# Setup and first attention in one block, scores kept in PSUM, one copy and one cast changed

## The reference

```python
mod = silu(c) @ ada_w.T + ada_b
shift_msa, scale_msa, gate_msa, shift_mlp, scale_mlp, gate_mlp = split(mod, 6, axis=1)
h = layernorm(x) * (1 + scale_msa[:, None]) + shift_msa[:, None]
q, k, v = heads(h @ qkv_w.T + qkv_b)               # 16 heads of 16
attn = where(mask_q & mask_k, q @ k.T * 16**-0.5, -1e9)
x = x + gate_msa[:, None] * (softmax(attn) @ v @ proj_w.T + proj_b)
h = layernorm(x) * (1 + scale_mlp[:, None]) + shift_mlp[:, None]
x = x + gate_mlp[:, None] * (gelu(h @ fc1_w.T + fc1_b) @ fc2_w.T + fc2_b)
# second block: shift from cond, attention with 16 heads of 64 and normed q and k,
# then 8 experts of 1024 hidden units, each over its top 1024 tokens
```

## Time and profile before

| what | value |
|---|---|
| median of 3 runs | 2549.15 us (2547.28 to 2550.14) |
| the profiled execution | 2552.78 us, of which 2550.9 us from first to last instruction |
| busy: PE, DVE, ACT, POOL | 2365.1, 1935.8, 1555.7, 1093.7 us |
| mean granted TensorE clock | 0.959 of full speed |
| setup, until its barrier | 0 to 29.4 us |
| attention0 | 29.4 to 510 us |

### The profile page before, as it was taken

One profiled execution on the slowest core, in us unless ns is written; L12 is line 12 of the kernel. 1 busy time (PEld: TensorE's weight loads), 2 busy tenths in 40 slices (PEclk: granted clock), 3 DMA queues, 4 the chain that ended last, 5 costly groups with the idle time before them and its releaser, 6 DMA issues. The chain is left out here.

```text
span 2550.9 us, 67195 instructions
## 1 busy us (share of the span) xinstructions
PE 2365.1 (93%) x24912; PEld 2075.8 (81%) x24912; DVE 1935.8 (76%) x3769; ACT 1555.7 (61%) x2979; POOL 1093.7 (43%) x939
## 2 busy tenths in 40 slices
PE   4999999889999979999999999999999825999997
PEld 3788888679999958888888888888888714999996
DVE  4899999656667668888888888888888767666663
ACT  3888888656666646566556555555555544655553
POOL 3799999700000024434434434434433303355543
PEclk8999999889999989999999999999999957999999
DMA  4111110011011000000000000000000022244322
GB/s 127 37 37 37 38 40 31 24 26 32 21 31 31 29 34 18 16 15 14 16 16 12 16 16 12 16 16 12 16 16 12 18 58 68 68 95 94 91 53 33
DMA packets 86352, 89.21 MB, mean 35 GB/s; under 512 B 26752, under 2 KB 80640, under 8 KB 83584
## 3 DMA queue, kind: packets, MB, share of 16 engines
q1 hardware_dynamic: 73984, 71.10, 9.0%
q0 software_dynamic: 12288, 17.05, 4.1%
HBM read 62.42 MB, written 25.69 MB: 35 GB/s over the span
## 5 line engine op out<-in xcount | busy, mean ns | idle before, releaser
L1050 POOL TENSOR_TENSOR a_rq<-a_vq,minus_half 128x8 f32<-128x8 f32 x256 | 417.3, 1639 | 98.6 <-DVE a_vq L1075 98.6
L994 ACT ACTIVATE a_sq<-a_bqk 128x512 f32<-128x512 f32 x256 | 152.9, 597 | 349.1 <-PE a_bqk L126 349.1
L1045 POOL TENSOR_TENSOR a_rstd<-a_veps,minus_half 128x1 f32<-128x1 f32 x64 | 35.3, 552 | 617.1 <-DVE a_veps L1119 617.1
L124 PE MATMUL a_bqk<-wqk_hi,a_h_lo 128*128 128x512 f32 x512 | 208.5, 407 | 5.1 <-DVE a_h_lo L1091 5.1
L126 PE MATMUL a_bqk<-wqk_hi,a_h_hi 128*128 128x512 f32 x512 | 201.7, 394 | 0.0
L125 PE MATMUL a_bqk<-wqk_lo,a_h_hi 128*128 128x512 f32 x512 | 201.7, 394 | 0.0
L1067 DVE TENSOR_TENSOR a_qk<-a_bqk,a_rq 128x512 f32<-128x512 f32 x256 | 176.0, 688 | 29.7 <-POOL a_rq L1050 29.6
L1812 DVE TENSOR_TENSOR e_u_lo<-e_u,e_u_hi 128x512 fp32r<-128x512 f32 x128 | 88.8, 695 | 127.2 <-ACT e_u_hi L1675 126.5
L1670 ACT ACTIVATE e_u<-e_bu,e_b 128x512 f32<-128x512 f32 x128 | 88.3, 690 | 156.8 <-PE e_bu L126 154.9
L981 ACT COPY a_vs<-a_ba 64x512 f32<-64x512 f32 x256 | 148.8, 581 | 53.7 <-PE a_ba L126 48.9
L1059 DVE TENSOR_REDUCE a_ss<-a_sq 128x8 f32<-128x512 f32 x256 | 174.2, 680 | 2.8 <-ACT a_sq L994 1.0
(11 more groups left out here) (284 smaller groups left out, 8150.7 us busy)
## 6 DMA issues: line engine op xcount, KB each, us to landing
X<-in_x SPq DMA_DIRECT2D x64, 128.0 KB, 2.1
a_gate<-gates_of_rows SPq DMA_DIRECT2D x128, 64.0 KB, 2.5
m_gate<-gates_of_rows SPq DMA_DIRECT2D x32, 256.0 KB, 4.1
tokens<-a_xs SPq DMA_DIRECT2D x64, 128.0 KB, 1.7
out<-a_xs SPq DMA_DIRECT2D x64, 128.0 KB, 1.7
e_w<-in_fc1s SPq DMA_DIRECT2D x8, 1024.0 KB, 5.1
e_w<-in_fc2s SPq DMA_DIRECT2D x8, 1024.0 KB, 4.8
wst<-in_qkv_w SPq DMA_DIRECT2D x16, 128.0 KB, 2.5
```

Of the source, the lines that this page charges most:

```text
L124: tensor.matmul(to, w_lo, x_hi, start=start, stop=False)
L994: nc.scalar.activation(sq[:, n * BK:(n + 1) * BK], b_qk[:, n * BK:(n + 1) * BK], ACT.Square).then_inc(s["sq"], 1)
L1050: nc.gpsimd.tensor_tensor(rq[:, 8 * n:8 * n + 8], vq[:, 8 * n:8 * n + 8], g.mhalf[:, 0:8], ALU.pow).then_inc(s["rq"], 1)
```

## The change

`setup_phase` is gone; its work is in `attention0_phase`, with semaphores of its own for each load.
- SP loads in the order of need: cond, the first two of six parts of `wada`, x of tiles 0 to 3 in one DMA, weights of q, k, v, constants, the projection's weights, the mask, x of tiles 4 to 7, then the rest of `wada`, `wada1` and the biases, then x of tiles 8 to 13. The mask is stored as 2 rows of 4096 bytes, each spread over 64 partitions.
- The four tables of the first attention are made ahead of step 0, each in a PSUM bank of its own; the other six and the gates at step 0, after the v product, in the banks of `a_bpt`, `a_bo` and of the scores.
- DVE makes `mrow` and `hide` at step -2, and `hidden` in eight pieces of one operation, four at step -1 and four at step 0. `vbB` and `pbB` come at steps 3 and 4, the low part of the weights of q, k, v at step -3, that of the projection's at POOL's step 1.
- Several tiles share memory: `wada` and the gate bias lie where `a_PT` and the next phase's first weights come later (`late`), cond in `a_qT`, the mask in `a_kbd`, the gates in the output tiles.
- The masked sum is written back to the score tile in PSUM, and `max` and subtract read it there; only the subtract writes `a_p`. PE's next score product waits for `shifted`, not for `scored`.
- `a_h_hi` is made by `reduce_max` over an axis of one element, not by a copy.
- ACT's output copy stands in the step of its projection, behind the second half of `a_PT`.

```diff
--- before.py
+++ after.py
...
-def setup_phase(nc, a, g):
...
+        late = m.sb("a0_late", [P, 4 * D * VB])
...
+        PT = late[:, 0:H * P].rearrange("p (n j q) -> p n j q", n=2, j=H // 2)
...
+        wada = late[:, 0:DC * 6 * D].rearrange("p (c m) -> p c m", c=DC)
+        wada1 = late[:, DC * 6 * D:DC * 7 * D].rearrange("p (c m) -> p c m", c=DC)
+        gbias, gates = late[:, DC * 7 * D:DC * 8 * D], tmps
+        cT, sT = (qT[:, n, :, 0:B] for n in range(2))
+        mask_keys = kbd[:, :, :, :].rearrange("p c j q -> p (c j q)").bitcast(U8).rearrange("p (t k) -> p t k", t=NT)
...
+        FIRST = 2 * DC
...
+        banks = [b_pt, b_o, b_q, b_k]
+        table_bank = [banks[n] if n < FIRST else banks[n % 2] for n in range(len(jobs))]
...
+                sp.dma_start(cT, a["condT"]).then_inc(s["in_c"], 16)
+                sp.dma_start(wada[:, :, 0:2 * D], a["ada_w"][:, :, 0:2 * D]).then_inc(s["in_wada"], 16)
+                sp.dma_start(adab[:, :], a["ada_b"]).then_inc(s["in_b"], 16)
+                sp.dma_start(g.X[:, 0:FEW, :], a["x"][0:FEW].rearrange("t p d -> p t d")).then_inc(s["in_x0"], 16)
+                sp.dma_start(g.wqkv0, a["qkv0_w"]).then_inc(s["in_wqkv"], 16)
+                sp.dma_start(g.cst, a["consts"]).then_inc(s["in_consts"], 16)
+                sp.dma_start(g.wproj0, a["proj0_w"]).then_inc(s["in_wproj"], 16)
+                sp.dma_start(g.qkb0, a["qk0_b"]).then_inc(s["in_qk"], 16)
+                sp.dma_start(mask_rows[:, :], a["maskT"]).then_inc(s["in_mask"], 16)
+                for b in range(2):
+                    sp.dma_start(mask_keys[b * S:(b + 1) * S, :, :],
+                                 a["mask"][b:b + 1].to_broadcast([S, NT, S])).then_inc(s["in_mask"], 16)
+                sp.dma_start(g.X[:, FEW:2 * FEW, :], a["x"][FEW:2 * FEW].rearrange("t p d -> p t d"))\
+                    .then_inc(s["in_x1"], 16)
+                sp.dma_start(wada[:, :, 2 * D:], a["ada_w"][:, :, 2 * D:]).then_inc(s["in_wada_rest"], 16)
+                sp.dma_start(wada1, a["ada1_w"]).then_inc(s["in_wada_rest"], 16)
...
+                for t in range(2 * FEW, AHEAD):
                     load_x(t)
+                sp.wait_ge(s["gate_out"], 2)
+                sp.dma_start(g.gate_dram, gates[:, :]).then_inc(s["gate_saved"], 16)
+                sp.wait_ge(s["gate_saved"], 16)
...
-                    if has(-7):
-                        act.wait_ge(s["proj"], i - 6)
-                        if later(i - 7):
-                            act.wait_ge(s["p1"], i - 7)
-                        nc.scalar.copy(tmp[:, :], b_pj[:, 0:D]).then_inc(s["proj_out"], 1)
...
+                    if has(-6):
+                        act.wait_ge(s["proj"], i - 5)
+                        if isinstance(i, int) and i == 6:
+                            act.wait_ge(s["gate_saved"], 16)
+                        if has(-7):
+                            act.wait_ge(s["p1"], i - 6)
+                        nc.scalar.copy(tmp[:, :], b_pj[:, 0:D]).then_inc(s["proj_out"], 1)
...
-                        nc.vector.tensor_copy(h_hi[:, (turn + 2) // 2 % 2, :, at], hT[:, :, at]).then_inc(s["h_hi"], 1)
+                        nc.vector.reduce_max(h_hi[:, (turn + 2) // 2 % 2, :, at], hT[:, :, at].unsqueeze(3), AX)\
+                            .then_inc(s["h_hi"], 1)
...
-                        if has(-6):
-                            dve.wait_ge(s["pT"], 2 * (i - 5))
+                        scores = b_s[:, :].rearrange("p (h k) -> p h k", h=H)
                         nc.vector.scalar_tensor_tensor(
-                            pa, b_s[:, :].rearrange("p (h k) -> p h k", h=H), g.mrow[:, bass.ds(i - 2, 1)],
+                            scores, scores, g.mrow[:, bass.ds(i - 2, 1)],
                             g.hidden[:, i - 2, :].unsqueeze(1).to_broadcast([P, H, S]),
                             ALU.mult, ALU.add).then_inc(s["scored"], 1)
                         dve.wait_ge(s["scored"], i - 1)
-                        nc.vector.reduce_max(mx[:, :], pa, AX).then_inc(s["maxed"], 1)
+                        nc.vector.reduce_max(mx[:, :], scores, AX).then_inc(s["maxed"], 1)
                         dve.wait_ge(s["maxed"], i - 1)
-                        nc.vector.tensor_tensor(pa, pa, mx[:, :].unsqueeze(2).to_broadcast([P, H, S]),
+                        if has(-6):
+                            dve.wait_ge(s["pT"], 2 * (i - 5))
+                        nc.vector.tensor_tensor(pa, scores, mx[:, :].unsqueeze(2).to_broadcast([P, H, S]),
                                                 ALU.subtract).then_inc(s["shifted"], 1)
                     if isinstance(i, int) and i == -4:
+                        tables(0, FIRST)
+                    if isinstance(i, int) and i == -3:
                         dve.wait_ge(s["own_hi"], 1)
                         nc.vector.tensor_tensor(wqkv_lo, g.wqkv0, wqkv_hi.bitcast(F32), ALU.subtract)\
                             .then_inc(s["own_lo"], 1)
...
+                    if isinstance(i, int) and i == -2:
+                        dve.wait_ge(s["in_mask"], 48)
+                        nc.vector.tensor_scalar(g.mrow, mask_rows[:, :], 1.0, None, ALU.mult).then_inc(s["hide"], 1)
+                        nc.vector.tensor_scalar(hide[:, :], mask_rows[:, :], -HIDE, None, ALU.mult)\
+                            .then_inc(s["hide"], 1)
+                        dve.wait_ge(s["hide"], 2)
+                    if isinstance(i, int) and -1 <= i < 1:
+                        for n in range(4 * (i + 1), 4 * (i + 2)):
+                            part = slice(n * (NT // 8), (n + 1) * (NT // 8))
+                            nc.vector.scalar_tensor_tensor(
+                                g.hidden[:, part, :], mask_keys[:, part, :], -1.0,
+                                hide[:, part].unsqueeze(2).to_broadcast([P, NT // 8, S]), ALU.add, ALU.mult)\
+                                .then_inc(s["hidden"], 1)
+                    if isinstance(i, int) and i == 0:
+                        dve.wait_ge(s["in_b1"], 64)
+                        nc.vector.tensor_tensor(shb[:, :], bada1[:, :], ln1b[:, :], ALU.add).then_inc(s["shb"], 1)
+                        dve.wait_ge(s["shb"], 1)
+                        tables(FIRST, len(jobs))
+                        for j in range(2):
+                            dve.wait_ge(s["gate_mm"], j + 1)
+                            nc.vector.tensor_tensor(gates[:, j * D:(j + 1) * D], b_s[:, 512 * j:512 * j + D],
+                                                    gbias[:, j * D:(j + 1) * D], ALU.add).then_inc(s["gate_out"], 1)
+                    if isinstance(i, int) and i == 3:
+                        dve.wait_ge(s["in_vb"], 32)
+                        for c in range(DC):
+                            last = nc.vector.tensor_copy(vbB[:, c, :], g.vb0[:, c:c + 1].to_broadcast([P, P]))
+                        last.then_inc(s["vb"], 1)
+                    if isinstance(i, int) and i == 4:
+                        dve.wait_ge(s["vb_mm"], 1)
+                        nc.vector.tensor_tensor(pbB[:, :], b_pj[:, 0:D], g.pb0, ALU.add).then_inc(s["pb"], 1)
...
+                def tables(first, end):
...
+                        if n >= FIRST:
+                            pe.wait_ge(s["table_out"], max(FIRST, n - 1))
+                        for kc in range(DC):
+                            w = wada1[:, kc, c * P:(c + 1) * P] if k is None else \
+                                wada[:, kc, k * D + c * P:k * D + (c + 1) * P]
+                            last = nc.tensor.matmul(table_bank[n][:, 0:P], w, sT[:, kc, :],
+                                                    start=(kc == 0), stop=(kc == DC - 1))
+                        last.then_inc(s["table_mm"], 1)
...
-                            pe.wait_ge(s["scored"], i - 2)
+                            pe.wait_ge(s["shifted"], i - 2)
...
+                    if isinstance(i, int) and i == 0:
+                        pe.wait_ge(s["in_wada_rest"], 32)
+                        tables(FIRST, len(jobs))
+                        for j, k in enumerate((2, 5)):
+                            for kc in range(DC):
+                                last = nc.tensor.matmul(b_s[:, 512 * j:512 * j + D], sT[:, kc, :],
+                                                        wada[:, kc, k * D:(k + 1) * D],
+                                                        start=(kc == 0), stop=(kc == DC - 1))
+                            last.then_inc(s["gate_mm"], 1)
...
-        "mask": mask,
+        "mask": np.ascontiguousarray(mask.reshape(NT, 2, S).swapaxes(0, 1)),
```

More of the change, by code:

```diff
@@ L420, in step @@
                         last.then_inc(s["q_out"], 2)
+                    if isinstance(i, int) and i == -1:
+                        act.wait_ge(s["in_wproj"], 16)
+                        nc.scalar.copy(wp_hi[:, :, :], g.wproj0).then_inc(s["own_hi"], 1)
+                        act.wait_ge(s["in_qk"], 16)
                     if isinstance(i, int) and i == NT + 2:
@@ L461, in step @@
```

(22 more changed lines are left out.)

199 lines of the change are left out of this document (62 added, 137 removed).

## The result

The changed kernel takes 2519.32 us (median of 4 runs, 2517.26 to 2519.58), beside 2548.22 us (2546.72 to 2550.14) for the kernel before on the same chip: a ratio of 0.988 with a 95% interval of 0.987 to 0.990, 28.9 us less. The forecast was 2519.6. The profiled execution took 2519.51 us, of which 2517.7 is the span.

A forecast was written before the change was run, and what follows sets the result against it. DVE was taken to bound the long stretch at 6.85 us a tile, PE next at 6.61. Fill 16 us plus stretch 0.24 us x 56 = 13.5 make 29.5: 2549.15 - 29.5 = 2519.6 us, range 2508 to 2534.

The forecast's parts named there:

- The bound of the stretch: Long stretch: DVE leads at 6.85 us a tile; after the change PE leads at 6.61, DVE at 6.43.
- The sum: Whole kernel: 16 us from the fill plus 13.5 from the stretch, 29.5 us less, 2519.6 us.
- `a_h_hi` as a reduction: DVE in the long stretch: the slot falls from 0.69 to 0.34 us, 0.35 us less a tile.
- rival B: Long stretch: the reduction needs two cycles an output, DVE at 6.70 us, gain 8.4, time 2525; chance 0.12.
- Scores in PSUM: Long stretch: DVE's subtract 0.07 us shorter a tile, masked sum as now, POOL falls to about 6 us.
- rival C: Long stretch: the masked sum in one bank goes at half rate, 1.28 becomes 2.35 us, time 2572; chance 0.07.
- Rival A: Long stretch: POOL's lock moves on to `a_xhat`, 0.47 us a tile, DVE at 6.9, time 2533; chance 0.17.
- The fill: Setup joined with the fill: tile work starts 26.3 us earlier, 14.3 put back, partly hidden; gain 16 us (12 to 19).
- The value bias and its product: Fill, steps 3 and 4 on DVE and PE: cost about 1 us or nothing, taken within the 16.
- The drain: End of the phase: counted at nothing, gain 0 to 2 us, the output copy no longer behind a weight cast on ACT.
- Rival D: Fill: the last table or gate arrives late and the fill keeps its length, time 2535; chance 0.04.

The follow-up runs named there:

- the kernel with the stretch's edits alone: Kernel before, setup phase kept, with ACT's copy moved, `a_h_hi` as a reduction and scores in PSUM: 2532.67 us against 2548.16, ratio 0.994.
- v1: Changed kernel with the value bias's work moved: DVE spreads `vb` in step 1, PE multiplies it ahead of step 3's score product: 2514.70 us, ratio 0.987.
- A alone: Changed kernel with `a_h_hi` a cast again and scores through SBUF again; of the stretch's edits only ACT's moved copy stays: 2531.52 us, ratio 0.994.
- without P: Changed kernel with scores written to SBUF again, read there by max and subtract, PE's score product waiting for `scored`: 2525.23 us, ratio 0.990.
- v3: v1 with two later tables ahead of the first v product, gates in step 1, raw mask in another buffer, its pieces spread: 2508.73 us, ratio 0.985.

## Why the prediction was right, step by step

**The bound of the stretch: right.** PE could do a tile in 6.61 us by the earlier trace rows; it does it in 6.600, and PE's wait came back as 0.19 us a tile when the copy went back. The other two bounds were near as well: DVE has 0.23 us a tile of waiting for PE left, so 6.37 for the 6.43 of the sum, and POOL two waits for DVE of 0.33 and 0.39, so about 5.9 for 6. The sum took 0.24 x 56 = 13.5 us; the kernel with the stretch's edits alone gained 15.5. The term was a little small, since some tiles before and behind that of the earlier trace rows were slower than 6.85: four early intervals between score products took 7.18 to 7.30 us and the late ones 6.93 to 6.95.

**`a_h_hi` as a reduction: the slot was right, its part in the sum wrong.** It goes from start to start in 0.33 us (205.30 to 205.63), as taken from the earlier trace rows, so rival B is out. But I credited it with 0.35 of the 0.42 us by which DVE was to get shorter. The kernel with the cast shows that this was the PSUM edit's doing: what held the cast off was POOL's late rhythm behind its long addition; with that gone the cast takes 285 ns. I had priced the two edits one by one from a tile in which both illnesses stand, and they had one cause.

**Scores in PSUM: right in sign, far too small.** Taken as -0.07 us a tile on the subtract and "POOL gains more". Undoing it alone costs 0.11 us a tile (6.710), and with the cast it is 0.25. The masked sum in its own bank takes 1293 ns for 1284, max 1225, subtract 1225: rival C is out. By the Trainium skill's errata rule (VectorE: DVE Perf Modes, § The TRN2 errata) max and subtract would each take 65 ns longer for their PSUM source. The rows show 5 ns (1220 to 1225) and none: the subtract from SBUF takes 1.22 us too where no POOL instruction runs beside it (at 58.98 us of the kernel before).

The Trainium skill (SBUF — State Buffer, § Who interferes with whom) also says that a DVE instruction with two SBUF inputs contends with a GpSimd instruction that reads SBUF, and one with a single SBUF input doesn't. The trace agrees: 1505 and 1567 ns for the pair with both inputs in SBUF, 1225 and 721 with the scores in PSUM. I had used this page for the cast and missed it for the edit on which it bears most.

**Rival A, the lock on `a_xhat`: out.** 0.40 us in the stretch, in every tile. In the fill it did happen, where POOL's work runs beside it. The argument that DVE comes first wants a lead, too. Over all traces of this phase, `a_xhat` took 0.88 to 0.96 us in the 15 cases in which a POOL instruction started 0.01 or 0.08 us behind it, and 0.40 to 0.42 in all those in which it started 0.11 to 0.17 behind; in the stretch of the kernel after the lead is 0.16. DVE in the kernel after:

```profile
15.62 0.84 DVE L467 TENSOR_SCALAR a_xhat<-X,a_mv,a_rstd 128x256 f32<-128x256 f32 x1
...
17.96 0.96 DVE L467 TENSOR_SCALAR a_xhat<-X,a_mv,a_rstd 128x256 f32<-128x256 f32 x1
...
35.48 1.53 DVE L467 TENSOR_SCALAR a_xhat<-X,a_mv,a_rstd 128x256 f32<-128x256 f32 x1
```

**The fill: about the right sum from wrong terms.** The parts, in DVE's timeline of the kernel after:

```profile
8.34 0.43 DVE L474 BATCH_NORM_STATS2 a_st<-X 128x6 f32<-128x256 f32 x1 [8.34 <-DMA X<-in_x]
...
19.67 2.49 DVE L514 SCALAR_TENSOR_TENSOR hidden<-a_kbd,a_hide 128x512 f32<-128x512 uint8 x4
...
26.22 0.35 DVE L434 TENSOR_SCALAR shift_mlp<-a_bpt,a_adab 128x128 f32<-128x128 f32 x1
```

- x was there at 8.34 us, not at 6 (5 to 8): its issue on SP is the fourth, at 2.77 us, and it landed 5.6 us later. The start of the tile work moved by 24.0 us, not 26.3.
- The mask's pieces took 5.0 us (twice 2.49), not 5.6. The six tables and two gates took from 26.22 to 31.49, 5.3 us, not 6.8: PE had started at 25.06, so that one was done and the second begun when DVE came.
- Put back, on the way to the first score product, were 5.4 us (24.0 less 18.6), where 14.3 was the sum without cover and 10.3 with what I took as hidden. The cover was better than I thought: DVE's pieces ran (19.67 to 22.16 and 23.56 to 26.05 us) beside PE's k and v products at the low rate. The first score product, forecast at 38 to 41 us, came at 36.7.
- **The step that failed** is "The value bias and its product, moved into steps 3 and 4 on DVE and PE, cost about 1 us or nothing". It cost 4.6 us by the time and 6.4 in the traces (12.90 less 6.54), with the low rate that goes with it. I priced its two instructions and not its place: a wait of PE on DVE behind the longest chain of DVE's step, though the prediction names just such a queue for the tables.

18.57 less the 3.83 given back by the fifth product are 14.7 us, against 16 taken (12 to 19). That it lies in the range is in part luck: two errors offset each other. Without the stall, in v1, the fifth score product comes 21.7 us earlier than before (60.28 for 81.97), beyond the range. The kernel with A alone, whose stretch is the old one, gained 17.8. Stretch and fill alone gain 15.5 and 17.8, together 28.9; the missing 4.4 are, as far as the traces show, mostly that stall. The old stretch takes it up in part: behind it the kernel with A alone runs five intervals at 6.60 us and reaches its last score product 3.0 us sooner after the fifth than the kernel before; the new stretch is at 6.60 anyway. How much of it each would hide in any one execution isn't settled, since PE's rate in the fill differs among them.

**The drain:** last score product to POOL's last addition 26.6 us before, 24.9 now: 1.7, within 0 to 2. **Rival D** is out.

**The sum** was 29.5 for 28.9 measured. In the traces the fill is 1.3 us under its 16 and the stretch, 59 periods from the fifth score product to the last, 1.3 over its 13.5. That they cancel is luck, and so in part is the agreement with the medians: these differ by 28.9 us, the two profiled executions by 33.2 in span.

## What to carry to other kernels

When several engines are nearly full, measure each one's own bound and expect the longest to count: single edits here were worth 0 to 4 us in the stretch, the right pair 15. Keep one input of a long two-input DVE operation out of SBUF where GpSimd reads SBUF beside it; that alone may make other cures needless. When setup work is spread into a filling pipeline, price the place of each piece by who waits behind it, and put it where the waiting engine idles anyway: the same instructions cost 4.6 us in one step and nothing in another.

## What the runs showed of the hardware

A reduction over an axis of one element takes 0.41 us for 256 columns beside GpSimd or not (in the kernel after at 205.30 and at 22.07 us); a cast takes 285 ns undisturbed and 754 where GpSimd's product with the gate has started ahead of it.

In the fill PE's steps between products are 0.21 us in every kernel from the first k product on, and 0.12 later, as at 1.2 and at 2.4 GHz; yet in some traces the granted clock of those microseconds reads 0.50 and in others 1.00. Windows of 18.80 to 21.40 us, first the kernel after, where it reads 0.50:

```profile
18.80:21.40 2.60, 2.58 (x12) 2.58 (x12) 2.43 (x7) 0.25 (x1) 0.93 (x1) 0.50 0.66 178
```

And v3, where PE's k products run at the same steps of 0.21 us:

```profile
18.80:21.40 2.60, 2.60 (x14) 2.60 (x14) 2.43 (x7) 0.42 (x2) 1.56 (x3) 1.00 0.55 144
```

The second 1.00 isn't a measured clock. The trace of v3 has its first entry for the clock at 21.43 us (the kernel after at 10.34), and a stretch without an entry is printed as 1.00; so is most of the setup in the earlier trace rows, since the first entry of the kernel before is at 23.03. At the start of a program the steps between like matmuls tell the rate, not the printed clock. Kernels with the same order of work up to there reached 0.12 at different times: the one without P from its v product at 22.7 us on, the changed kernel only at its q product, 30.7. What decides it stays open.
